# Reading each tile's head stacks in two halves instead of one piece, in the cross-attention of a decoder layer

## The chip, the cores and the metric

The kernel runs on one core of a Trainium2 chip. The metric is the device time of one execution in microseconds, as the median of several runs. TensorE does matrix products and transposes, VectorE, ScalarE and GpSimd (POOL in the profile) work element by element, and SyncE (SP) issues every transfer between the chip's memory (DRAM scratch arrays here) and SBUF.

## The reference, cut to what matters

One decoder layer on x of 16 x 256 x 512 in float32: a windowed self-attention, a cross-attention with a context of the same shape, and a mixture of experts. The change lies in the cross-attention:

```python
x = x + _L0_xattn_ref(_layernorm(x, axis=-1), ctx_2048, ctx_2048, L0_xattn_gamma)

def _L0_xattn_ref(q, k, v, gamma):
    N_HEAD = 8
    B, Dq, Lq = q.shape            # 16, 256, 512
    h = N_HEAD
    dq = Dq // h                   # 32
    qh = q.reshape(B, h, dq, Lq)
    kh = k.reshape(B, h, dq, Lk)
    vh = v.reshape(B, h, dv, Lk)
    qk = jnp.einsum('bhdq,bhdl->bhql', qh, kh) * scale
    sm = jax.nn.softmax(qk, axis=-1)
    ret = jnp.einsum('bhql,bhdl->bhdq', sm, vh)
    return gamma * ret.reshape(B, Dv, Lq)
```

The position axis (256) plays the part of the channels: a head is 32 rows of a sequence, and the scores of a head are a 512 x 512 matrix.

## The kernel before

The stage works on 32 tiles of 128 rows by 512 columns, which are four heads each (XPT = 4, XD = 32). A float32 product is made of rounded parts: ScalarE rounds queries and keys (`q_round`, `k_round`), GpSimd forms the rests (`q_rest`, `k_rest`), and rounded part and rest lie in `qp` and `kp`. To contract all products of the parts in one matmul, the parts of a head's 32 rows are stacked on 96 partitions. That move goes through DRAM: `write_queries` and `write_keys` write a tile's parts to `sq_scratch` and `sk_scratch` (512 KB each), and `read_stacks` reads them back into `qst` and `kst`, [partitions, 4 heads, 512], in six transfers of 256 KB; each writes 32 of the partitions, every third one, for all four heads. There are three stack buffers (STACKS = 3). Rows 96 and 97 of `qst` take the negated maxima of the scores, also as part and rest, which `max_rows` copies there in two transfers of 8 KB.

TensorE makes every score twice. `scores` (L782) makes them for the maxima, which VectorE takes (L928); `transposed_scores` (L791) makes them again, transposed, with the maxima subtracted by the two extra rows, and ScalarE takes their exponentials (L868). `weigh` (L802) multiplies by the values `vt`, and `sums` (L812) adds up the denominators. The loop on TensorE runs over steps, four to a tile, and four heads or chunks to a step; the scores run six steps (AHEAD = 6) ahead of the transposed scores. So the scores of tile n+2, first head, stand at the middle of tile n, and those of its third head at the start of tile n+1. Behind the first scores of tile n+2 in the same queue stand the transpose of the maxima of tile n+1 (L819) and all the rest of tile n. Only the first scores of a tile wait for the stacks:

```python
if h == 0 and q == 0:
    pe.wait_ge(s_st[m % STACKS], 16 * 2 * PARTS * (m // STACKS + 1))
```

SyncE issues its transfers in one order, and each waits for its turn in that order. For tile n of the loop this is: `read_stacks(n + 2)`, when the writes of that tile have landed and the transposed scores of tile n-1 are done (this frees the buffer); `write_queries(n + 3)`, `write_keys(n + 3)`, `load_values(n + 2)`, `load_context(n + 4)` (`cin`), `load_x(n + 5)`, and last `max_rows(n + 1)`, which waits for ScalarE's `xmhi` (L889). The transposed scores of tile n+1 wait for these rows at the tile's start.

Of the kernel before, what the change touches and what calls it, by code (L numbers as in the profile page):

```python
# [5 lines left out]
F32 = mybir.dt.float32  # L6
# [586 lines left out]
def cross_attention(nc, x1, ctx_in, ctx_t, gamma, sq, sk, mv2, mv3, x2, cst):  # L593
# [4 lines left out]
    with ctx:  # L598
        def sb(name, shape, dt):
            return ctx.enter_context(nc.sbuf_tensor(name, shape, dt))  # L600
# [4 lines left out]
        def sem(name):  # L605
            return ctx.enter_context(nc.semaphore(name))

        PARTS = 3
        KS = PARTS * XD
# [3 lines left out]
        STACKS = 3  # L613
# [11 lines left out]
        qst = [sb(f"qst{i}", [P, XPT, D], F32R) for i in range(STACKS)]  # L625
        kst = [sb(f"kst{i}", [P, XPT, D], F32R) for i in range(STACKS)]
# [20 lines left out]
        s_qn, s_qhi, s_qlo = sem("x_qn"), sem("x_qhi"), sem("x_qlo")  # L647
        s_khi, s_klo = sem("x_khi"), sem("x_klo")
        s_qw, s_kw = sem("x_qw"), sem("x_kw")
        s_st = [sem(f"x_st{i}") for i in range(STACKS)]  # L650
        s_row = [sem(f"x_row{i}") for i in range(STACKS)]
        s_ones = sem("x_ones")
        s_sc, s_mx = sem("x_sc"), sem("x_mx")
# [14 lines left out]
        def tile(n):  # L668
            return 0 <= n < TILES

        @block.sync
        def _(sp):
            sp.dma_start(gam[:, :], gamma.rearrange("(a b) -> a b", a=1).broadcast_to([P, 1])).then_inc(s_gam, 16)

            def load_x(m):
                sp.dma_start(x2[:, m, :], x1v[m // 2, m % 2]).then_inc(s_xi[m % 6], 16)

            def load_context(m):
                if m >= 4:
                    sp.wait_ge(s_klo, m - 3)  # L680
                sp.dma_start(cin[:, m % 4, :], cv[m]).then_inc(s_ci[m % 4], 16)

            def load_values(m):
                if m >= 3:
                    sp.wait_ge(s_pv, CB * (m - 2))
                sp.dma_start(vt[:, m % 3, :, :], ctx_t[m]).then_inc(s_vt[m % 3], 16)

            def write_queries(m):
                sp.wait_ge(s_qlo, m + 1)
                sp.dma_start(sq[m % 2].rearrange("h p d -> p h d"), qp[m % 2][:, :, :].bitcast(F32)).then_inc(s_qw, 16)  # L690

            def write_keys(m):
                sp.wait_ge(s_klo, m + 1)
                sp.dma_start(sk[m % 2].rearrange("h p d -> p h d"), kp[m % 2][:, :, :].bitcast(F32)).then_inc(s_kw, 16)

            def read_stacks(m):
                sp.wait_ge(s_qw, 16 * m + 16)
                sp.wait_ge(s_kw, 16 * m + 16)
                if m >= STACKS:
                    sp.wait_ge(s_ts, 16 * (m - STACKS) + 16)  # L700
                qv = sq[m % 2].rearrange("h (j r) d -> h r j d", j=XPT)
                kv = sk[m % 2].rearrange("h (j r) d -> h r j d", j=XPT)
                for c in range(PARTS):
                    rows = slice(c, KS, PARTS)
                    sp.dma_start(qst[m % STACKS][rows, :, :].bitcast(F32), qv[c // 2]).then_inc(s_st[m % STACKS], 16)
                    sp.dma_start(kst[m % STACKS][rows, :, :].bitcast(F32), kv[c % 2]).then_inc(s_st[m % STACKS], 16)

            def max_rows(m):
                for k, (part, here) in enumerate(((mhi, s_mhi), (mlo, s_mlo))):
                    sp.wait_ge(here, m + 1)  # L710
                    row = qst[m % STACKS][KS + k:KS + k + 1, :, :].rearrange("o h (q n) -> o (h q) n", n=P)
                    sp.dma_start(row.bitcast(F32), part[:, :].bitcast(F32)).then_inc(s_row[m % STACKS], 16)

            for m in range(4):
                load_x(m)
                load_context(m)
            load_x(4)
            for n in range(-3, TILES):
                if tile(n + 2):
                    read_stacks(n + 2)  # L720
                if tile(n + 3):
                    write_queries(n + 3)
                    write_keys(n + 3)
                if tile(n + 2):
                    load_values(n + 2)
                if n >= 0 and tile(n + 4):
                    load_context(n + 4)
                if n >= 0 and tile(n + 5):
                    sp.wait_ge(s_qn, n + 2)
                    load_x(n + 5)  # L730
                if tile(n + 1):
                    max_rows(n + 1)
# [41 lines left out]
        @block.tensor  # L774
        def _(pe):
            def scores(g, q):
                m, h = g // CB, g % CB
                if h == 0 and q == 0:
                    pe.wait_ge(s_st[m % STACKS], 16 * 2 * PARTS * (m // STACKS + 1))
                if 4 * g + q >= 2:  # L780
                    pe.wait_ge(s_mx, 4 * g + q - 1)
                nc.tensor.matmul(SC[q % 2][:, :], qst[m % STACKS][0:KS, h, q * P:(q + 1) * P],  # L782
                                 kst[m % STACKS][0:KS, h, :], start=True, stop=True).then_inc(s_sc, 1)

            def transposed_scores(s, h):
                n, c = s // CB, s % CB
                if c == 0 and h == 0:
                    pe.wait_ge(s_row[n % STACKS], 32 * (n // STACKS + 1))
                if 4 * s + h >= 2:
                    pe.wait_ge(s_exp, 4 * s + h - 1)  # L790
                nc.tensor.matmul(ST[h % 2][:, :], kst[n % STACKS][0:KM, h, c * P:(c + 1) * P],  # L791
                                 qst[n % STACKS][0:KM, h, :], start=True, stop=True).then_inc(s_ts, 1)

            def weigh(s):
                n, c = s // CB, s % CB
                pe.wait_ge(s_exp, 4 * s + 4)
                pe.wait_ge(s_vt[n % 3], 16 * (n // 3 + 1))
                if c == 0:
                    pe.wait_ge(s_oe, n)
                for h in range(XPT):  # L800
                    rows = slice(XD * h, XD * (h + 1))
                    last = nc.tensor.matmul(OB[rows, :], vt[:, n % 3, c, rows], prt[s % RING][:, h, :],  # L802
                                            start=(c == 0), stop=(c == CB - 1))
                last.then_inc(s_pv, 1)

            def sums(n, k):
                pe.wait_ge(s_add, XPT * (2 * n + k + 1))
                if k == 0 and n >= 2:
                    pe.wait_ge(s_on, n - 1)
                for h in range(XPT):  # L810
                    rows = slice(XD * h, XD * (h + 1))
                    last = nc.tensor.matmul(SU[n % 2][rows, :], ones[:, :], prt[(CB * n + 2 * k) % RING][:, h, :],  # L812
                                            start=(k == 0), stop=(k == 1))
                last.then_inc(s_su, 1)

            def max_transposes(n):
                pe.wait_ge(s_mx, 16 * n + 16)
                pe.wait_ge(s_mlo, n)
                nc.tensor.transpose(MX[0:XPT * CB, 0:P], nmx[:, n % 2, :], ident[:, :]).then_inc(s_mt, 1)  # L819

            pe.wait_ge(s_ones, STACKS + 1)
            for s in range(FIRST, LAST):
                for i in range(XPT):
                    if 0 <= s + AHEAD < STEPS:
                        scores(s + AHEAD, i)
                    if 0 <= s < STEPS:
                        transposed_scores(s, i)
                    if i == 1 and s % CB == 2 and tile(s // CB + 1):
                        max_transposes(s // CB + 1)
                    if i == 1 and 0 <= s - 1 < STEPS:  # L830
                        weigh(s - 1)
                if s % CB in (0, 2) and tile(s // CB - 1):
                    sums(s // CB - 1, s % CB // 2)
# [597 lines left out]
```

## Time and profile before

| | |
|---|---|
| time, median of 3 runs | 2736.11 us (2734.95 to 2745.65) |
| profiled execution | 2744.02 us, its span 2742.3 us, mean granted clock 0.976 |
| TensorE matmuls busy | 2591.8 us, 95% of the span |
| VectorE, ScalarE, GpSimd busy | 65%, 35%, 31% of the span |
| cross-attention, 1984 to 2512.5 us | 528.5 us: TensorE 499.8 busy, VectorE 409.3, GpSimd 408.1, ScalarE 362.1; transfer engines busy 0.62, 198 GB/s |

Read the table from below: the stage is a fifth of the time, every engine in it is under its full load, and TensorE is nearest to it. The durations in the trace come from the one profiled execution, which was 8 us longer than the median of the others.

### The profile page before, as it was taken

What the parts mean: (1) busy time and instruction counts of PE and PEld (TensorE: products, weight loads), DVE (VectorE), ACT (ScalarE), POOL (GpSimd) and SP (SyncE); (2) the same over time, 40 slices, a digit from 0 to 9 for tenths busy, and PEclk for the clock granted to TensorE, in tenths of its full rate; (3) what the DMA queues carried; (4) which work ended last, traced back from release to release, by engine and by line L of the source; (5) the groups of instructions that cost most, each with busy time, mean ns of one, the idle gap of its engine ahead of it and who ended that gap; (6) DMA issues with size and microseconds to landing.
All of it is one profiled execution on the core that took longest, in us unless ns stands there. A gap on an engine that the chain in (4) does not pass through costs nothing. (4 is left out here: it accounts for less than half of the span.)

```text
span 2742.3 us, 37159 instructions
## 1 busy us (share of the span) xinstructions
PE 2591.8 (95%) x12936; PEld 1920.3 (70%) x12936; DVE 1794.3 (65%) x3705; ACT 968.3 (35%) x2435; POOL 861.5 (31%) x698
## 2 busy tenths in 40 slices
PE   6999999999999999999999999999499999999794
PEld 5888888888888888888887888888343333333583
DVE  5777776655665566565565666566478777776657
ACT  2322223322222332222232222222257776776220
POOL 3211112321111222121132212111258888887000
PEclk9999999999999999999999999999789999999897
DMA  3123323222211222221122321110466666662003
GB/s 115 62 81 103 111 91 123 77 77 92 93 62 62 97 74 86 99 77 62 62 100 70 101 99 62 62 62 32 140 200 213 211 214 202 204 198 71 20 1 123
DMA packets 167078, 280.58 MB, mean 102 GB/s; under 512 B 12016, under 2 KB 78576, under 8 KB 166896
## 3 DMA queue, kind: packets, MB, share of 16 engines
q1 hardware_dynamic: 166896, 278.21, 30.3%
q8 instruction: 107, 1.75, 0.3%
q14 instruction: 75, 0.61, 0.1%
HBM read 185.37 MB, written 92.27 MB: 101 GB/s over the span
## 5 line engine op out<-in xcount | busy, mean ns | idle before, releaser
L324 PE MATMUL pj<-xnt,whi 128*128 128x512 f32 x2048 | 706.9, 407 | 4.4 <-DVE xnt L558 4.4
L417 ACT ACTIVATE pr<-sc,nmx 128x128 f32<-128x128 f32 (+1 forms) x512 | 211.1, 417 | 930.0 <-DVE nmx L503 930.0
L269 POOL TENSOR_TENSOR qt<-rot,swp 128x512 f32<-128x512 f32 x128 | 166.0, 1297 | 1107.8 <-DVE swp L483 1107.8
L324 PEld LDWEIGHTS pj<-xnt,whi 128*128 128x128 f32 x2048 | 387.5, 189 | 97.6 <-DVE xnt L558 5.2
L928 DVE TENSOR_REDUCE xnmx<-xsc 128x1 f32<-128x512 f32 x512 | 336.4, 684 | 125.5 <-PE xsc L782 122.1
L324 PE MATMUL pj<-xnt,wlo 128*128 128x512 f32 x1024 | 400.2, 391 | 0.0
L321 PE MATMUL pj<-whi,xnt 128*128 128x512 f32 x1024 | 352.8, 406 | 4.0 <-issue 4.0
L752 POOL TENSOR_TENSOR xprt<-xprt 128x512 f32<-128x512 f32 x256 | 320.2, 1283 | 103.6 <-PE xob L802 103.6
L868 ACT ACTIVATE xprt<-xst 128x512 f32<-128x512 f32 x512 | 291.8, 596 | 158.0 <-PE xst L791 156.7
L481 DVE TENSOR_TENSOR rot<-pj,trig 128x512 f32<-128x512 f32 x256 | 176.7, 690 | 213.7 <-PE pj L324 213.7
L782 PE MATMUL xsc<-kst,qst 96*128 96x512 f32 x512 | 241.6, 476 | 56.7 <-DMA kst<-sk_scratch 51.7
L782 PEld LDWEIGHTS xsc<-kst,qst 96*128 96x128 f32 x512 | 99.5, 195 | 265.9 <-DVE xnmx L928 184.2
L269 POOL TENSOR_TENSOR kt<-rot,swp 128x512 f32<-128x512 f32 x128 | 165.1, 1290 | 308.1 <-DVE swp L483 308.1
L512 DVE TENSOR_SCALAR pr<-pr,rinv 128x128 f32<-128x128 f32 (+1 forms) x512 | 253.2, 535 | 9.0
L503 DVE TENSOR_REDUCE nmx<-sc 128x1 f32<-128x128 f32 (+1 forms) x512 | 158.3, 351 | 146.3 <-PE sc L358 141.9
L321 PEld LDWEIGHTS pj<-whi,xnt 128*128 128x128 f32 x1024 | 193.2, 189 | 50.5 <-issue 4.3
L324 PEld LDWEIGHTS pj<-xnt,wlo 128*128 128x128 f32 x1024 | 194.9, 190 | 34.7
L345 PE MATMUL pj<-whi,ohi 128*128 128x512 f32 x512 | 212.4, 415 | 1.4 <-DVE olo L517 1.4
L791 PE MATMUL xst<-qst,kst 98*128 98x512 f32 x512 | 209.7, 412 | 3.0 <-ACT xprt L868 1.4
L491 DVE TENSOR_TENSOR xio<-pj,xio 128x512 f32<-128x512 f32 x128 | 88.5, 692 | 180.6 <-PE pj L345 180.6
L345 PE MATMUL pj<-whi,olo 128*128 128x512 f32 x512 | 201.6, 394 | 0.0
L321 PE MATMUL pj<-wlo,xnt 128*128 128x512 f32 x512 | 199.8, 390 | 0.0
(183 smaller groups left out, 4230.6 us busy)
## 6 DMA issues: line engine op xcount, KB each, us to landing
xnt<-xt_scratch SPq DMA_DIRECT2D x48, 1024.0 KB, 7.0
x_scratch<-xio SPq DMA_DIRECT2D x64, 512.0 KB, 3.6
xio<-x_scratch SPq DMA_DIRECT2D x48, 512.0 KB, 4.0
qst<-sq_scratch SPq DMA_DIRECT2D x96, 256.0 KB, 4.2
kst<-sk_scratch SPq DMA_DIRECT2D x96, 256.0 KB, 4.7
raw<-in_w_all_dram SPq DMA_DIRECT2D x64, 256.0 KB, 4.7
xt_scratch<-xnt SPq DMA_DIRECT2D x16, 1024.0 KB, 8.9
sq_scratch<-qp SPq DMA_DIRECT2D x32, 512.0 KB, 6.1
```

The source lines that it names most:

```text
L269: nc.gpsimd.tensor_tensor(qk["QK".index(kind)][h][:, :, :].rearrange("p b n -> p (b n)"), rot[r % 2][:, :], swp[r % 2][:, :], ALU.add).the ...
L321: last = nc.tensor.matmul(bank[:, :], moving[:, i * P:(i + 1) * P], wpart[:, w, :], start=(k == 0), stop=(k == 3 * CB - 1))
L324: last = nc.tensor.matmul(bank[:, :], wpart[:, w, i * HD:(i + 1) * HD], moving, start=(k == 0), stop=(k == 3 * CB - 1))
L345: last = nc.tensor.matmul(PJ[n % 3][:, :], o[:, h, tok], w[:, CH_O + h, :], start=(h == 0 and k == 0), stop=(h == HG - 1 and k == 2))
L417: nc.scalar.activation(pr[:, a % 4, lo:hi], SC[a % 2][:, lo:hi], ACT.Exp, bias=nmx[:, a % 4, t:t + 1], accum_out=rsum[:, a % 4, t:t + 1]). ...
L481: nc.vector.tensor_tensor(ro, bank, table(slice(0, P), q), ALU.mult)
L512: nc.vector.tensor_scalar(pr[:, a % 4, lo:hi], pr[:, a % 4, lo:hi], rinv[:, a % 4, t:t + 1], None, ALU.mult).then_inc(s_pr, 1)
L752: nc.gpsimd.tensor_tensor(a[:, h, :], a[:, h, :], b[:, h, :], ALU.add).then_inc(s_add, 1)
L782: nc.tensor.matmul(SC[q % 2][:, :], qst[m % STACKS][0:KS, h, q * P:(q + 1) * P], kst[m % STACKS][0:KS, h, :], start=True, stop=True).then_ ...
L791: nc.tensor.matmul(ST[h % 2][:, :], kst[n % STACKS][0:KM, h, c * P:(c + 1) * P], qst[n % STACKS][0:KM, h, :], start=True, stop=True).then_ ...
L868: nc.scalar.activation(prt[s % RING][:, h, :], ST[h % 2][:, :], ACT.Exp).then_inc(s_exp, 1)
L928: nc.vector.tensor_reduce(nmx[:, m % 2, k:k + 1], SC[q % 2][:, :], AX.X, ALU.max, negate=True).then_inc(s_mx, 1)
```

## The change

`read_stacks` takes two halves of two heads each. A half is read in six transfers of 128 KB, twelve for a tile, and each half of each buffer has a semaphore of its own. `scores` waits for the first half at the first head of a tile and for the second at the third head. The bytes, their places and the size of a contiguous piece (512 values) stay.

```diff
-        s_st = [sem(f"x_st{i}") for i in range(STACKS)]
+        s_st = [[sem(f"x_st{i}{k}") for k in range(2)] for i in range(STACKS)]
...
-                for c in range(PARTS):
-                    rows = slice(c, KS, PARTS)
-                    sp.dma_start(qst[m % STACKS][rows, :, :].bitcast(F32), qv[c // 2]).then_inc(s_st[m % STACKS], 16)
-                    sp.dma_start(kst[m % STACKS][rows, :, :].bitcast(F32), kv[c % 2]).then_inc(s_st[m % STACKS], 16)
+                for k in range(2):
+                    heads, here = slice(2 * k, 2 * k + 2), s_st[m % STACKS][k]
+                    for c in range(PARTS):
+                        rows = slice(c, KS, PARTS)
+                        sp.dma_start(qst[m % STACKS][rows, heads, :].bitcast(F32), qv[c // 2][:, heads, :]).then_inc(here, 16)
+                        sp.dma_start(kst[m % STACKS][rows, heads, :].bitcast(F32), kv[c % 2][:, heads, :]).then_inc(here, 16)
...
-                if h == 0 and q == 0:
-                    pe.wait_ge(s_st[m % STACKS], 16 * 2 * PARTS * (m // STACKS + 1))
+                if h % 2 == 0 and q == 0:
+                    pe.wait_ge(s_st[m % STACKS][h // 2], 16 * 2 * PARTS * (m // STACKS + 1))
```

SyncE's queue in the steady state, before: the end of one tile's reads (32 partitions x 4 heads x 512), what stands behind them, and the first reads of the next tile. The names in brackets are the semaphores that a transfer waits for; `x_ts` counts transposed scores, `x_mhi` and `x_mlo` the maxima.

```order
L705 DMA qst<-sq_scratch 32x4x512
L706 DMA kst<-sk_scratch 32x4x512
L690 DMA sq_scratch<-qp 128x2x512 [waits x_qlo]
L694 DMA sk_scratch<-kp 128x2x512 [waits x_klo]
L686 DMA vt<-in_ctx_t_dram 128x512 [waits x_pv]
L681 DMA cin<-in_ctx_in_dram 128x512 [waits x_klo]
L676 DMA x<-x_scratch 128x512 [waits x_qn]
L712 DMA qst<-xmhi 1x16x128 [waits x_mhi]
L712 DMA qst<-xmlo 1x16x128 [waits x_mlo]
L705 DMA qst<-sq_scratch 32x4x512 [waits x_ts,x_kw,x_qw]
L706 DMA kst<-sk_scratch 32x4x512
```

The same place in the changed kernel:

```order
L707 DMA qst<-sq_scratch 32x2x512
L708 DMA kst<-sk_scratch 32x2x512
L690 DMA sq_scratch<-qp 128x2x512 [waits x_qlo]
L694 DMA sk_scratch<-kp 128x2x512 [waits x_klo]
L686 DMA vt<-in_ctx_t_dram 128x512 [waits x_pv]
L681 DMA cin<-in_ctx_in_dram 128x512 [waits x_klo]
L676 DMA x<-x_scratch 128x512 [waits x_qn]
L714 DMA qst<-xmhi 1x16x128 [waits x_mhi]
L714 DMA qst<-xmlo 1x16x128 [waits x_mlo]
L707 DMA qst<-sq_scratch 32x2x512 [waits x_ts,x_kw,x_qw]
L708 DMA kst<-sk_scratch 32x2x512
```

The order is the same, but twelve reads of two heads stand where six of four heads stood, so everything from the query write on has six more issues ahead of it.

TensorE's queue at the start of a tile, before (L782 scores, L791 transposed scores, L802 weighting; `x_row0` are the two copied rows of maxima):

```order
L782 MATMUL xsc<-kst,qst 128x512 [waits x_mx]
L791 MATMUL xst<-qst,kst 128x512 [waits x_exp,x_row0]
L782 MATMUL xsc<-kst,qst 128x512 [waits x_mx]
L791 MATMUL xst<-qst,kst 128x512 [waits x_exp]
L802 MATMUL xob<-xprt,vt 32x512 [waits x_vt2,x_exp]
```

The same place in the changed kernel, where every line number is two higher:

```order
L784 MATMUL xsc<-kst,qst 128x512 [waits x_mx,x_st11]
L793 MATMUL xst<-qst,kst 128x512 [waits x_exp,x_row0]
L784 MATMUL xsc<-kst,qst 128x512 [waits x_mx]
L793 MATMUL xst<-qst,kst 128x512 [waits x_exp]
L804 MATMUL xob<-xprt,vt 32x512 [waits x_vt2,x_exp]
```

Nothing moves on TensorE. The scores of the third head of a tile, which stand directly ahead of the transposed scores that open another tile, have a wait of their own now (`x_st11` is the second half of buffer 1).

## Rows read from the trace of the kernel before

**Rows 1.** The page: TensorE's busy tenths in 40 slices of the span.

```profile
PE   6999999999999999999999999999499999999794
```

**Rows 2.** Waits from 2012 to 2500 us: total us, times, longest.

```profile
PE xsc L782 <- DMA kst<-sk_scratch: 22.1, 28, 2.3
```

**Rows 3.** Timeline of TensorE: start, duration, instruction [idle time before it <- what ended it].

```profile
2210.26 0.50 PE L782 MATMUL xsc<-kst,qst 96*128 96x512 f32 x1 [0.33 <-DMA kst<-sk_scratch]
...
2218.37 0.39 PE L791 MATMUL xst<-qst,kst 98*128 98x512 f32 x1
...
2227.23 0.50 PE L782 MATMUL xsc<-kst,qst 96*128 96x512 f32 x1 [1.14 <-DMA kst<-sk_scratch]
...
2259.77 0.48 PE L782 MATMUL xsc<-kst,qst 96*128 96x512 f32 x1 [0.18 <-DVE xnmx L928]
...
2277.89 0.53 PE L782 MATMUL xsc<-kst,qst 96*128 96x512 f32 x1 [2.29 <-DMA kst<-sk_scratch]
...
2295.46 0.50 PE L782 MATMUL xsc<-kst,qst 96*128 96x512 f32 x1 [0.20 <-DMA kst<-sk_scratch]
...
2328.91 0.50 PE L782 MATMUL xsc<-kst,qst 96*128 96x512 f32 x1 [1.33 <-DMA kst<-sk_scratch]
```

**Rows 4.** Windows: length, busy by engine, granted clock, DMA share, GB/s.

```profile
2278.20:2281.60 3.40, 3.40 (x13) 1.00 (x11) 1.38 (x2) 1.20 (x2) 3.40 (x4) 0.50 0.40 155
2261.40:2264.80 3.40, 3.40 (x23) 1.39 (x16) 1.84 (x5) 1.57 (x4) 3.40 (x4) 1.00 0.61 229
```

**Rows 5.** Timeline of SyncE's queue over one tile: start of an issue, its duration.

```profile
2201.91 0.61 SPq L705 DMA_DIRECT2D qst<-sq_scratch  x1
...
2205.13 0.60 SPq L706 DMA_DIRECT2D kst<-sk_scratch  x1
2205.78 0.59 SPq L690 DMA_DIRECT2D sq_scratch<-qp  x1
2207.06 0.38 SPq L694 DMA_DIRECT2D sk_scratch<-kp  x1
2207.48 1.39 SPq L686 DMA_DIRECT2D vt<-in_ctx_t_dram  x1
2208.91 1.17 SPq L681 DMA_DIRECT2D cin<-in_ctx_in_dram  x1
2210.13 0.49 SPq L676 DMA_DIRECT2D x<-x_scratch  x1
2214.03 0.56 SPq L712 DMA_DIRECT2D qst<-xmhi  x1
2214.64 0.59 SPq L712 DMA_DIRECT2D qst<-xmlo  x1
...
2218.06 0.61 SPq L705 DMA_DIRECT2D qst<-sq_scratch  x1
```

**Rows 6.** Waits of SyncE's queue, 2012 to 2500 us.

```profile
SPq L712 <- ACT xmhi L889: 123.2, 29, 6.8
```

**Rows 7.** Windows of 2 us of the same tile, columns as in rows 4.

```profile
2201.90:2203.90 2.00, 1.95 (x8) 0.89 (x12) 2.00 (x4) 2.00 (x6) 2.00 (x3) 1.00 0.18 41
2203.90:2205.90 2.00, 2.00 (x16) 0.84 (x12) 1.90 (x5) 1.24 (x4) 2.00 (x3) 1.00 1.01 296
...
2211.90:2213.90 2.00, 2.00 (x16) 0.83 (x12) 0.88 (x2) 0.85 (x3) 2.00 (x3) 1.00 1.02 391
2213.90:2215.90 2.00, 2.00 (x16) 0.82 (x12) 1.61 (x4) 1.08 (x4) 2.00 (x3) 1.00 0.07 21
```

**Rows 8.** Transfers from 2012 to 2500 us: size, median us from issue to landing.

```profile
kst<-sk_scratch SPq DMA_DIRECT2D x87, 256.0 KB, 4.7
...
qst<-xmlo SPq DMA_DIRECT2D x29, 8.0 KB, 1.9
```

**Rows 9.** Timeline of SyncE's queue at the start of the stage.

```profile
1960.09 0.42 SPq L681 DMA_DIRECT2D cin<-in_ctx_in_dram  x1
```

**Rows 10.** Timeline of TensorE: the first scores of the stage.

```profile
1983.71 1.19 PE L782 MATMUL xsc<-kst,qst 96*128 96x512 f32 x2 [29.67 <-DMA kst<-sk_scratch]
```

## The prediction, made before the changed kernel ran

> **What bounds the kernel now.** I read the page first: TensorE is busy nearly everywhere, the cross-attention too [rows 1]. So only what makes TensorE stand still there, or lowers its clock, is worth time. The changed transfers exist only in that stage, and everything ahead of and behind it stays as it is.
>
> Next the waits between 2012 and 2500 us, where the stage is in its steady state. TensorE's matmuls stand still for one thing worth naming: scores (L782) that wait for the stacks, 22.1 us in 28 waits, 0.79 us each, at the first scores of a tile [rows 2].
>
> Then the timeline, one row per such place. Tile starts lie 16.97 us apart with a wait of 1.14 us at the end (2210.26 to 2227.23), so 15.83 us of work [rows 3]. Where the stacks were there in time, 0.18 us remained, charged to VectorE (2259.77). That is the floor: the wait can't fall below it. After the wait of 2.29 us at 2277.89 the next interval is 17.57 us, less its own wait of 0.20 still 17.37, so 1.54 us more than 15.83. The windows say why: from 2278.2 to 2281.6 the granted clock was 0.50 (the 1.2 GHz level) and TensorE retired 13 matmuls in 3.4 us, against 23 at 1.00 in an equal stretch of the tile before [rows 4]. The clock fell likewise behind the wait of 1.33 us at 2328.91 [rows 3] and behind one of 1.51 us at the stage's start: three times in all, each about 3.4 us long.
>
> Last SyncE's queue, for one tile. Let T be the issue of a tile's first stack read, 2201.91. The sixth is at T+3.2, one per 0.645 us; the query write at T+3.9, the key write at T+5.2, vt, cin and x up to T+8.7, then the queue idles until xmhi exists at T+12.1, and the next reads go at 2218.06 [rows 5]. SyncE waits 123.2 us in 29 waits for xmhi, 4.2 us per tile: that is the room in the queue [rows 6]. TensorE wants the first scores at about T+8.0 (2210.26 less 0.33) and gets them at T+8.3. The transfer engines carry almost nothing until T+2.0, are full from there to T+12.0, at 296 GB/s with stack reads in them and at 391 with the writes and plain loads behind them, and idle after it (share 0.07) [rows 7].
>
> **The change, step by step.**
>
> *First half earlier.* Today 1.57 MB are asked for within 3.9 us, 400 GB/s, and delivered at about 296, so the sixth read queues behind five others: issued at T+3.2, landed at T+8.3. The new first half is also six issues. No row shows a stack read of 128 KB. Its issue lies between 0.33 and 0.60 us: a plain load of 256 KB took 0.42 us on an empty queue and an 8 KB row copy 0.56 [rows 5, 9]; I take 0.60, since the small row copy hardly costs less than a large read. Then 128 KB per 0.645 us is 203 GB/s, under what the transfer engines deliver, and nothing queues. Data starts about 1.9 us after an issue (the engines are empty until T+2, and 8 KB land in 1.9 us [rows 7, 8]), takes 0.45 us at 296 GB/s and is signalled about a microsecond later: T+3.2+3.4 = T+6.6 at the latest likely, T+5.5 with quick issues. Both are ahead of T+8.0. The wait goes, down to the floor: 22.1 - 28 x 0.18 = **17.1 us**. A hiccup like the one at 2277.89 (2 us late) would still leave only some 0.5 us.
>
> *Clock.* With no wait over a microsecond in the middle of a tile the three slow stretches have no cause: 3 x 1.54 = **4.6 us**. Bounds 0 (they come anyway) and 4.6.
>
> *Second half.* Issued to T+7.7, landed near T+10.6. Scores of the third head are wanted eight scores later, half a tile, T+15.9 (the added wait stands right there, with transposed scores and weighting queued behind it). Free by 5 us.
>
> *What is queued behind on SyncE.* Six more issues of 0.645 us: 3.9 us, bounds 0.6 (twelve of 0.33 + 0.045 against 3.9) and 3.9. The key write also waited for GpSimd, 2207.06 instead of 2206.4, and now finds kp ready. vt and cin took 1.39 and 1.17 us to issue while the transfer engines were full and 0.42 when they were empty [rows 5, 9]; how much of that comes back I leave at nothing to 1.7 us. SyncE is then done with x at T+10.2 to T+12.2. xmhi exists at about T+11.3 (T+12.1 less the removed wait). The row copies are issued at most 1 us late.
>
> *What is queued behind on the transfer engines.* The stack reads end at T+7.7+1.9 = T+9.5 in place of about T+7.4; 1.84 MB of writes and loads at 400 GB/s take 4.6 us, so all is drained at **T+14.1** where it was T+12.0. The row copies now go into queues that are still full and land near T+15.2; today they land at 2214.64+1.9 = T+14.6 [rows 5, 8]. The transposed scores of the next tile want them at 15.83+0.3 = **T+16.1** (2218.37 against the reads at 2218.06 [rows 3, 5]). Margin 0.9 us; landings of today scatter by about that, so I book 0.07 us a tile, **2 us**. The key write, issued at T+8.4, has 1.05 MB ahead and in it: T+9.5+2.6+1.2 = T+13.3, and the next reads need it at T+15.8. cin lands near T+15 and is rounded in the next tile, behind exponentials of its first step, past T+16. Free.
>
> *Start of the stage.* The very first scores wait until 1983.71 for six whole reads [rows 10]; they come 1.7 us sooner. But each next tile's reads there wait for a write that is now issued 3.9 us later (by as much, less some of the queueing), so tile 1 starts no sooner, and the first row copies queue behind a write. Bounds -1.7 and +4; I take **+1 us**.
>
> Sum: -17.1 - 4.6 + 2 + 1 = -18.7 us on the profiled 2744.0, 2725.3 or -0.68%. The median of the runs shown is 8 us below the profiled run, and I can't tell whether it had the three slow stretches; without them the gain is 14.1. On the median I take **17 us, 2719**.
>
> **A rule against it.** The rows show 8 KB landing after 1.9 us and whole reads, six in flight, after 4.7 [rows 8]: small ones are not slow here. The Trainium skill (DMA: Bandwidth & Descriptors, section Bandwidth) says to batch transfers to 1 MiB and more, and gives 0.95 us of busy transfer time for 64 KB against 6.15 for 1 MB. An estimate between its figures is 2.0 us for 256 KB and 1.3 for 128 KB, so 3.6 us more per tile if they ran one after the other; the drain would come at about T+15.6 and the rows half a microsecond late. By that the gain would be some 4 us only. The trace speaks against it: six reads landed 8.3 us after the first issue, not twelve.
>
> **The rivals.**
>
> *A. The rows are late, and it is slower (chance 0.14).* Each half costs the transfer engines far more than half a read, so they stay full from T+2 on. Place: the wait of the transposed scores for the row copies. It decides from a landing at T+16.9 on (T+16.1 plus the 0.77 us a tile gained), that is a drain 1.7 us after my T+14.1, or stack reads at about 170 GB/s. If a half cost as much as a whole, 0.88 us, reads would take 10.6 us, the rows land at T+18.2 and tiles last 17.9 us where they last 15.83+0.79 = 16.6: 29 x 1.3, about +38 us. At 160 GB/s the rows land at T+17.5 and the tile is 17.2 us: +17 us, 2753. For it: 2 KB packets into 32 partitions already run at 296 where others run at 400. Against: the packets keep their size.
>
> *B. The rows take back part (0.20).* Lands between T+16.2 and T+16.8: 0.1 to 0.6 us a tile, 3 to 17 us; 2722 to 2736, most near 2729.
>
> *C. The stacks are no sooner (0.06).* Landing is latency and not queueing: then the first half still comes at T+3.2+4.7 = T+7.9, and the gain is 0 to 6 us: 2730 to 2736. The 1.9 us of the row copies speak against it.
>
> *D. The forecast (0.60):* 2712 to 2725.
>
> **Numbers.** The range 2711 to 2738 holds D, B and C and leaves A. What a measurement can tell from no change is about 0.5%, 13.7 us, so faster means below 2722.4: most of D (0.51) and a little of B, 0.53; slower means above 2749.8: most of A, 0.12; between them 0.35.
>
> **What would show it.** The matmul wait for the stacks falls from 22.1 us to under 6; stack reads land in about 3.4 us; SyncE's reads keep a pitch of 0.6 to 0.65 us; its wait for xmhi shrinks from 4.2 to under 1 us; the row copies land later than 1.9 us; the interval of tiles is 16.0 us; no stretch at half clock from 2012 to 2500. Wrong if transposed scores (L791 before) wait for row copies at tile starts, if the halves' pitch is over 0.75 us, or if stack reads land no sooner.

## The result and the profile after

The changed kernel took 2724.77 us (median of 5 runs, 2723.01 to 2726.1) against 2736.11 us before (median of 5, 2733.56 to 2745.65): a ratio of 0.9953, 95% interval 0.9937 to 0.9969. It is faster by 11.3 us, a little under half a per cent. The profiled executions are further apart: 2725.4 us (span 2723.6) against 2744.0, which is 18.6 us. The prediction called it faster below 2722.4 us, with a chance of 0.53; the time fell just above that, where the chance of 0.35 lay.

The waits between 2012 and 2500 us, the view of [rows 2] for the changed kernel (line numbers are two higher, so L784 are the scores and L793 the transposed scores):

```profile
PE xsc L784 <- DVE xnmx L930: 10.2, 60, 0.5
...
PE xst L793 <- DMA qst<-xmlo: 2.0, 4, 1.0
```

No wait of TensorE for the stacks is left in the stretch, neither at the first nor at the third head; it was 22.1 us. What remains ahead of the scores are 60 waits of 0.17 us put down to VectorE, half of them at the first head of a tile and half at the third, where the kernel before had none. The second kind costs nothing that can be seen: a tile lasts 16.03 us, as it does with four stack buffers (below), which has them at the first head alone. A new wait has come, 2.0 us in all, for the copied rows of maxima.

SyncE's queue over one tile, the view of [rows 5], from T = 2195.24:

```profile
2195.24 0.60 SPq L707 DMA_DIRECT2D qst<-sq_scratch  x1
...
2202.28 0.60 SPq L708 DMA_DIRECT2D kst<-sk_scratch  x1
2202.92 0.59 SPq L690 DMA_DIRECT2D sq_scratch<-qp  x1
...
2206.25 0.50 SPq L676 DMA_DIRECT2D x<-x_scratch  x1
2207.25 0.56 SPq L714 DMA_DIRECT2D qst<-xmhi  x1
2207.85 0.59 SPq L714 DMA_DIRECT2D qst<-xmlo  x1
2211.27 0.60 SPq L707 DMA_DIRECT2D qst<-sq_scratch  x1
```

A read of half the bytes takes as long to issue, 0.60 us, one per 0.64. The query write goes at T+7.7 where it went at T+3.9, the rows at T+12.0, and the next reads after 16.03 us. Half a microsecond is left between the end of the x issue and the rows; it was 3.4. SyncE's waits for xmhi in the stretch fell from 123.2 us to 30.0, and 14.4 of these are a single wait.

The transfers of the same stretch, as in [rows 8], size and median us to landing:

```profile
kst<-sk_scratch SPq DMA_DIRECT2D x174, 128.0 KB, 2.6
...
qst<-xmlo SPq DMA_DIRECT2D x31, 8.0 KB, 3.3
```

The reads land in 2.6 us where they took 4.7; the rows land in 3.3 us where they took 1.9. Both come from the load on the transfer engines, and the windows of 2 us show it (columns of [rows 4], the third figure from the right is the clock, the last the GB/s):

```profile
2195.20:2197.20 2.00, 1.85 (x8) 0.86 (x12) 1.95 (x4) 2.00 (x6) 2.00 (x3) 1.00 0.21 70
2197.20:2199.20 2.00, 2.00 (x16) 0.84 (x12) 1.97 (x5) 1.24 (x4) 2.00 (x3) 1.00 0.66 193
...
2201.20:2203.20 2.00, 2.00 (x12) 0.70 (x7) 1.74 (x3) 1.65 (x4) 0.96 (x1) 1.00 0.75 208
...
2205.20:2207.20 2.00, 2.00 (x16) 0.83 (x12) 0.73 (x2) 0.93 (x4) 2.00 (x3) 1.00 1.03 351
2207.20:2209.20 2.00, 2.00 (x16) 0.83 (x12) 1.69 (x4) 1.08 (x4) 2.00 (x3) 1.00 1.01 331
2209.20:2211.20 2.00, 1.99 (x12) 0.68 (x4) 1.17 (x3) 1.45 (x4) 1.56 (x2) 1.00 0.23 82
```

While the halves are read the transfer engines are two thirds busy at 193 to 208 GB/s; before, they were full at 296 GB/s in the same place. Nothing queues, so a read lands soon. The writes and loads come later, so the engines are still full when the rows are asked for, at T+12.0 and T+12.6, and idle from about T+14.4.

### The profile page after: what moved, and what is told of

Its sections match the earlier page's. It is cut to its first block and busy times, and to the rows that moved or that the text cites. A ratio compares the mean times of both kernels' runs of the same rounds, so it can differ in the third digit from the quotient of the medians.

```text
span 2723.6 us, 37383 instructions
## 1 busy us (share of the span) xinstructions
PE 2586.9 (95%) x12936; PEld 1918.0 (70%) x12936; DVE 1794.5 (66%) x3705; ACT 964.9 (35%) x2435; POOL 861.5 (32%) x698
## 5 line engine op out<-in xcount | busy, mean ns | idle before, releaser
L784 PE MATMUL xsc<-kst,qst 96*128 96x512 f32 x512 | 238.6, 470 | 39.9 <-DMA kst<-sk_scratch 27.4
L784 PEld LDWEIGHTS xsc<-kst,qst 96*128 96x128 f32 x512 | 99.1, 194 | 247.6 <-DVE xnmx L930 172.2
L793 PE MATMUL xst<-qst,kst 98*128 98x512 f32 x512 | 208.8, 411 | 4.9 <-DMA qst<-xmlo 2.9
```

## The experiments

Ratios are to the kernel before, run beside each kernel on the same chip; "stage" is the time from the first scores to the start of the last transposed scores in the profiled execution.

| kernel | median us | before, same chip | ratio, 95% interval | stage us |
|---|---|---|---|---|
| before, unchanged | 2738.57 | 2741.0 | 0.9989, 0.998 to 0.9998 | 543.0 |
| halves, one signal | 2800.68 | 2741.0 | 1.022, 1.0205 to 1.0236 | 603.3 |
| three parts | 2809.47 | 2741.0 | 1.0248, 1.0234 to 1.0262 | 617.3 |
| writes between the halves | 2721.09 | 2741.0 | 0.9929, 0.9916 to 0.9941 | 527.0 |
| smaller rings (control) | 2733.41 | 2739.56 | 0.9985, 0.9973 to 0.9996 | 538.0 |
| four stack buffers | 2722.34 | 2739.56 | 0.9939, 0.9923 to 0.9954 | 527.2 |
| second half before the rows | 2722.31 | 2739.56 | 0.9935, 0.9917 to 0.9954 | 529.2 |
| changed kernel again | 2724.98 | 2738.6 | 0.9949, 0.9931 to 0.9967 | 529.8 |
| writes between, again | 2720.35 | 2738.6 | 0.993, 0.9911 to 0.9949 | 527.4 |
| four stack buffers, again | 2720.9 | 2738.6 | 0.9932, 0.9914 to 0.9949 | 528.4 |

The stage was 548.4 us in the first trace of before and 530.5 in that of the changed kernel. (The stretch of 528.5 us in the table of the kernel before ends at 2512.5 us; the last transposed scores start at 2532.1.) The stage as measured here leaves out how long the first scores wait for their reads; that comes under the reasons below. The first row is a yardstick too: the same kernel against itself came out at 0.9989, so a difference of a part in a thousand, 2.7 us, is not to be read in this table.

**The kernel before, traced once more.** No edit. 

> The kernel before, unchanged, for a second trace of it. The first trace, of an execution of 2744.0 us, lies 8 us over the median, and the changed kernel gained 18.7 us on it but 11.3 us on the median. Theory: the waits for the stacks are about the same in every execution (17 to 24 us in 28 waits between 2012 and 2500 us), and it is the slow stretches of TensorE's clock behind some of them (three, 4.6 us) that come and go; so an execution near the median shows none or one. Rival: the waits themselves vary from run to run, and a quick execution shows 8 to 15 us of them.

Measured: the profiled execution took 2734.0 us, and in the same stretch:

```profile
PE xsc L782 <- DMA kst<-sk_scratch: 18.1, 25, 2.4
```

18.1 us of waits, and no stretch at half clock in 2012 to 2500 us, where the first trace had 22.1 us and three. The stage was 5.4 us shorter and began 4.1 us sooner. The theory holds as to the clock; the waits differ by 4 us too. So the loss by slow stretches is a loss of some executions. The two traces lie on either side of the middle: the first, on which the sum was made, was of a long execution, this one of the quickest of its ten (median 2738.57).

**One signal for both halves.** The twelve smaller reads stay, and the first head waits for all of them, so what is taken away is the first half's own signal.

```diff
-                if h % 2 == 0 and q == 0:
-                    pe.wait_ge(s_st[m % STACKS][h // 2], 16 * 2 * PARTS * (m // STACKS + 1))
+                if h == 0 and q == 0:
+                    for k in range(2):
+                        pe.wait_ge(s_st[m % STACKS][k], 16 * 2 * PARTS * (m // STACKS + 1))
```

> The changed kernel with its twelve transfers of 128 KB, but the scores of a tile's first head wait for both halves (as before, one point of waiting a tile). Theory (what counts is that the first half is signalled by itself): the twelfth read is issued 7.0 us after the first and lands 2.6 us later, at T+9.6 to T+10; TensorE wants it at T+8.0, so it stands 1.6 to 2 us in each of 28 tiles, 45 to 56 us, and slow stretches of the clock of 1.5 us each come behind some of them: 2765 to 2815 us. Rival (small transfers alone bring it, since nothing queues): 2723 to 2730 us, with waits under 6 us.

Measured 2800.68 us, 59.7 us above the kernel before. The wait is where the theory puts it, and the reads land as in the changed kernel:

```profile
PE xsc L785 <- DMA kst<-sk_scratch: 55.1, 26, 2.9
...
qst<-sq_scratch SPq DMA_DIRECT2D x156, 128.0 KB, 2.6
```

55.1 us in 26 waits, 2.1 us each. Twelve stretches at half clock, each 3.4 us, lie behind them; at 1.5 us each, an estimate from the three of the first trace, they make some 18 us more. Twelve smaller transfers under one signal cost 60 us here, since the twelfth is issued only 7.0 us after the first. The signal of the first half makes up for that loss and brings all of the gain.

**Three parts.** First head, second head, then two heads; a signal for each.

```diff
-                for k in range(2):
-                    heads, here = slice(2 * k, 2 * k + 2), s_st[m % STACKS][k]
+                for k, heads in enumerate((slice(0, 1), slice(1, 2), slice(2, 4))):
+                    here = s_st[m % STACKS][k]
```

> Three parts in place of two: first head, second head, third and fourth, six transfers each, eighteen a tile, a signal for each part. Theory (the price is SyncE's issue, about 0.64 us whatever the size, and the row copies behind it): eighteen reads take 11.5 us, what stands behind them 5 us, so the row copies are issued from T+15 on and land near T+19, and a tile lasts 18.5 to 19 us in place of 16.0: 2795 to 2815 us, with waits of the transposed scores for qst<-xmlo of 2.5 to 3 us a tile. Rival (bytes are what counts, the issue is cheap for smaller reads or hidden): 2720 to 2730 us.

Measured 2809.47 us, inside the expected 2795 to 2815. The issue is the price: a read of 64 KB took 0.59 us to issue at the median, as one of 256 KB, and it landed in 2.2 us.

```profile
PE xst L793 <- DMA qst<-xmlo: 48.0, 16, 4.4
...
qst<-sq_scratch SPq DMA_DIRECT2D x157, 64.0 KB, 2.2
```

The shape of the loss was not as expected. It is not 2.5 to 3 us at each tile but 3.0 us at 16 places in 26 tiles, every other tile mostly: tiles of 16.0 us alternate with tiles of 20 to 22 us, and behind the long waits the clock is down. Timeline of SyncE's queue over a long tile, and two windows of TensorE around its end:

```profile
2197.37 0.51 SPq L707 DMA_DIRECT2D qst<-sq_scratch  x1
...
2213.48 0.57 SPq L714 DMA_DIRECT2D qst<-xmhi  x1
2214.09 0.59 SPq L714 DMA_DIRECT2D qst<-xmlo  x1
2214.79 0.52 SPq L707 DMA_DIRECT2D qst<-sq_scratch  x1
```

```profile
2214.00:2218.00 4.00, 0.00 (x0) 0.00 (x0) 1.28 (x2) 0.49 (x1) 3.23 (x3) 0.69 0.74 246
2218.40:2222.40 4.00, 4.00 (x13) 1.50 (x14) 1.30 (x2) 1.60 (x3) 1.27 (x1) 0.51 0.38 98
```

SyncE issues with no wait for 17.4 us, longer than a tile of 16.0: it is itself what bounds the long tile. The late rows hold TensorE back by some 4 us, and with that lead SyncE is in time for the next tile, so every other tile is short: over the stretch SyncE still stands 49 us in 35 waits. The rows are asked for 16.1 us after the tile's first read. TensorE starts no matmul from 2214 to 2218, and then runs 13 in 4 us at a granted clock of 0.51.

**Writes between the halves.** First half, writes of queries and keys, second half; one wait keeps the scratch from being overwritten.

```diff
             def write_queries(m):
                 sp.wait_ge(s_qlo, m + 1)
+                if m >= 2:
+                    sp.wait_ge(s_st[(m - 2) % STACKS][1], 16 * 2 * PARTS * ((m - 2) // STACKS + 1))
...
                 if tile(n + 2):
-                    read_stacks(n + 2)
+                    read_stacks(n + 2, 0)
                 if tile(n + 3):
                     write_queries(n + 3)
                     write_keys(n + 3)
+                if tile(n + 2):
+                    read_stacks(n + 2, 1)
```

> The changed kernel with the writes of queries and keys issued between the two halves, so that the first reads and the writes stand in the queue where they stood before; the write of the queries waits also for the second half of two tiles earlier, which has long landed. Theory: in the steady state nothing changes (tiles of 16.0 us; second half landed by T+13, wanted at T+15.9), at the start of the stage the reads of tile 1 begin about 3 us sooner and the first row copies are not late: 1 to 3 us less than the changed kernel, 2721.5 to 2724. Rival (the row copies and the second half then queue behind the writes on the transfer engines, and the second half comes late): waits at L782's third head or for qst<-xmlo, 2728 to 2745 us.

Measured 0.9929 of the kernel before, and beside the changed kernel on one chip 2720.35 against 2724.98 us: 4.6 us less, somewhat more than expected. What the traces show of it lies at the start of the stage. The changed kernel's timeline of TensorE there:

```profile
1995.60 1.22 PE L784 MATMUL xsc<-kst,qst 96*128 96x512 f32 x2 [0.45 <-DMA kst<-sk_scratch]
...
2003.73 0.80 PE L793 MATMUL xst<-qst,kst 98*128 98x512 f32 x1 [0.95 <-DMA qst<-xmlo]
```

And the same two places in the kernel before:

```profile
1996.39 1.30 PE L782 MATMUL xsc<-kst,qst 96*128 96x512 f32 x2 [0.28 <-DVE xnmx L928]
...
2003.28 0.63 PE L791 MATMUL xst<-qst,kst 98*128 98x512 f32 x1
```

With the writes between, neither wait is there (one of 0.5 us, in the repeat of 0.3 us, for the second half of tile 0 has come), and the steady waits for the rows (5.2 us on the weight-load side in the second trace of the changed kernel) are down to 1.7 us in the repeat, which follows.

> The writes between the halves, again, beside the changed kernel on the same chip. If the start of the stage gains, 1 to 3 us below the changed kernel, with the stage (first scores to last transposed scores) at 527 us against 530.5. Rival: the two are the same within 1 us, and the lower time came from the chip it ran on.

The stage of 527.4 against 529.8 and 530.5 us agrees. The traced execution of the changed kernel was the quickest of its six, 2.1 us below their median. So the two traces are only 2.2 us apart, and from the first scores to the third transpose of the maxima the kernel with the writes between is 2.2 us quicker (43.2 against 45.4). The rest of the 4.6 us is in no trace and stays open.

**Four stack buffers, and its control.** Six whole reads and one signal, as before the change. The memory comes from one buffer less for the exponentials and two less for the context, which the control has as well.

```diff
-        RING = 6
-        STACKS = 3
+        RING = 5
+        STACKS = 4
...
-        cin = sb("cin", [P, 4, D], F32)
+        cin = sb("cin", [P, 2, D], F32)
```

> Control for the next kernel: the kernel before (six transfers of 256 KB, three stack buffers) with five in place of six buffers for the exponentials and two in place of four for the context, loads of the context issued later at the start. These give the memory that a fourth stack buffer takes. Expected of either theory: like the kernel before, 2732 to 2742 us, with the waits for the stacks at about 0.6 to 0.8 us a tile.

> The control with four stack buffers, six whole transfers of 256 KB and one signal. The reads no longer wait for the transposed scores of the tile before to free a buffer; SyncE issues them behind the row copies, about 3 us sooner. Theory (the waits are the time between a freed buffer and a landed read, too long by 0.3 to 2.3 us; either an earlier start or a shorter landing removes them): waits for the stacks under 6 us, tiles of 16.0 us, no slow stretch, row copies landed in 1.9 us: 12 to 20 us less than the control, 2717 to 2725 us, at least as good as the halves. Rival (splitting itself is what helps, the start is bound by something else such as the landing of the writes): the reads start hardly sooner, waits stay above 15 us, 2730 to 2740 us.

Measured: control 2733.41, four buffers 2722.34 us on the same chip, 11.1 us less, a little under the 12 to 20 expected. The control still waits; TensorE's matmuls have no wait for stacks or rows in the stretch at all with four buffers. The first row is of the control, the other two of the four buffers (transfers, then a wait of SyncE's queue):

```profile
PE xsc L782 <- DMA kst<-sk_scratch: 13.4, 24, 1.3
```

```profile
kst<-sk_scratch SPq DMA_DIRECT2D x87, 256.0 KB, 4.5
```

```profile
SPq L711 <- ACT xmhi L889: 154.3, 31, 14.4
```

The reads land hardly faster than before (4.5 us, it was 4.7); they start sooner, right behind the rows, and that is enough. So the stall was the distance from a freed buffer to landed stacks, and splitting is one of two cures. This one also leaves SyncE its room, 4.7 us a tile beside the one long wait of 14.4, and the rows land in 1.8 us.

> The four whole stack buffers again, beside the others. Steady tiles of 16.03 us as with the halves and a stage of 527 us, so 1 to 3 us below the changed kernel. Rival: the smaller rings for exponentials and context cost 1 to 3 us elsewhere, and it is level with it.

It came to 2720.9 us, 4.1 us below the changed kernel, and level with the writes between. Where the 4.1 us lie is not shown: the two traced executions are 0.6 us apart (2722.23 and 2722.87), the stage of 528.4 us is longer than the 527 expected, and its first scores come 8.6 us after the first read, as in the kernel before, where the changed kernel has 5.9.

**Second half behind writes and loads, just ahead of the rows.** The edit moves `read_stacks(n + 2, 1)` down to there.

> The changed kernel with the second half read behind the writes and the loads, just ahead of the row copies. Theory: first half and writes as early as before the change; the second half is issued from about T+7.5 to T+11.5 and lands near T+14, wanted at T+15.9; the start of the stage gains as in the kernel with the writes between: 2720 to 2725 us. Rival (the loads now run into the second half and it lands after T+16): waits of the third head's scores for the stacks, 0.5 to 2 us a tile, 2740 to 2780 us.

Measured 2722.31 us, ratio 0.9935: the theory as to the time and the steady tiles of 16.03 us. The gain at the start did not come with it. There the third head's scores of tile 0 wait for the second half, and the stage took 529.2 us, not 527:

```profile
1990.32 1.22 PE L788 MATMUL xsc<-kst,qst 96*128 96x512 f32 x2 [1.60 <-DMA kst<-sk_scratch]
```

The order of what stands behind the first half hardly matters, as long as all of it is issued before the rows are due.

**The changed kernel again.** 

> The changed kernel, unchanged, beside the two variants that came out lowest, all on one chip. Steady tiles of 16.0 us and row copies that land in about 3 us again. Theory (the changed kernel repeats itself within about 3 us, the kernel before scatters over 10 us, since its waits and slow clock stretches vary): 2722 to 2727 us against a kernel before at 2734 to 2742, a ratio of 0.993 to 0.9965. Rival (the first comparison was right to the tenth of a per cent): the ratio is 0.995 to 0.996 again.

Measured 2724.98 us (2722.87 to 2729.51) against 2738.6 (2733.46 to 2749.32), 0.9949. The changed kernel repeats its 2724.8 within its scatter of 7 us, the kernel before scatters over 16 us. The two pairs, 0.9953 and 0.9949, agree within their intervals, so this does not decide between theory and rival; a gain of 11 to 14 us is what both say.

## Why the prediction came out as it did

The mechanism was right, and so was the time in its range: 2724.77 lies at the upper edge of the forecast of 2712 to 2725, which had been given 0.60, and within rival B's 2722 to 2736 too. So it is the traces and not the time that tell which of the two it was. They are cut here at the first stack read of the stage, the first scores, and the transposes of the maxima, one a tile (L819 before, L821 changed):

| stretch, us | before | before, second trace | changed | changed, second trace |
|---|---|---|---|---|
| first stack read to first scores | 8.6 | 8.5 | 5.9 | 5.9 |
| from there to the third transpose | 44.9 | 46.4 | 45.3 | 45.4 |
| third to last transpose, 29 tiles | 484.7 | 477.9 | 465.1 | 465.7 |
| from there to the last transposed scores | 18.8 | 18.7 | 20.0 | 18.8 |
| sum | 557.0 | 551.5 | 536.3 | 535.8 |

*First half earlier: right, in every part.* The pitch of issues stayed at 0.64 us, the engines were off their limit at 203 GB/s as worked out (193 to 208), the reads landed in 2.6 us (3.4 assumed) and the wait fell to the floor of 0.17 us. The kernel with one signal shows that it is the first half's own signal that does it, that with four buffers that only the time of arrival counts. Rival C, landing as pure latency, is out: 4.7 us became 2.6. On the trace that the sum was made from, the steady part came out as booked: the 29 tiles are 19.6 us shorter, and the terms were -17.1 - 4.6 + 2 = -19.7.

*Clock and waits: the terms that were mis-sized for the median.* The 4.6 us and the 17.1 us were booked from one trace, of a long execution. The second trace of the kernel before has none of the three slow stretches and 18.1 us of waits in place of 22.1, and against it the 29 tiles are 12.2 to 12.8 us shorter. On the median the gain measured 11.3 and 13.6 us, where I said 17. I had noted that the median might lack the slow stretches and took a middle value; the lower one, 14.1, was nearer. The reason given, that waits over a microsecond cause the slow stretches, is too simple: in the first trace waits of 1.42 us (2194.12) and 1.26 us (2480.28) had none behind them, and in the second a wait of 2.39 us had none. What decides it stays open.

*The row copies: right in kind, nearer than thought.* The drain was to be at T+14.1 and was at about T+14.4; the rows were to land at T+15.2 and landed at T+15.9 at the median (2207.85 less 2195.24, and 3.3 us), so of the margin of 0.9 us 0.2 was left. TensorE's matmuls waited for them 2.0 us in the steady stretch and 2.8 us in the second trace; I had booked 2. By the prediction's own list such waits were a sign of being wrong. They did come, four in the stretch, one at the start and one at the end, and they were small. The writes and loads ran at 351 and 331 GB/s at their end, where the 391 of before had been taken; why is not shown. Rival B is this mechanism, and it stayed at the small end. Rival A did not happen: the engines were 0.66 to 0.75 busy while the halves were read, and not full. The three parts came to A's late rows and to its time by another way, the eighteen issues.

*Start of the stage: booked +1, and it gained.* The parts that were named are there: the scores of tile 1 wait 0.45 us and the first transposed scores 0.95 us, and the reads of tile 1 began 13.0 us after those of tile 0 where it was 11.2. But the first scores came 2.7 us sooner after the first read (2.5 against the second trace of before), not 1.7. The first read and the first scores, before and changed:

```profile
1975.09 0.65 SPq L705 DMA_DIRECT2D qst<-sq_scratch  x1
```

```profile
1976.80 0.65 SPq L707 DMA_DIRECT2D qst<-sq_scratch  x1
```

```profile
1982.68 1.19 PE L784 MATMUL xsc<-kst,qst 96*128 96x512 f32 x2 [26.92 <-DMA kst<-sk_scratch]
```

Before, the scores stood at 1983.71 [rows 10]. From the first read to the third transpose it took 51.2 us, against 53.6 and 54.8 before: a gain of 2.3 us or more where a loss of 1 was booked. Not foreseen: the last tile's rows are late by 1.0 us too, with a slow stretch of the clock behind it in that one execution; in the second trace they are late by 0.9 us with none.

*What of the agreement was luck.* The sum gave 2725.3 us for the profiled execution, and it took 2725.4. The steady part earned that. The rest cancelled out: the start gained 2.3 us in place of losing 1, the end lost 1.3 us that nobody had booked, and the time ahead of the first stack read, which the change does not touch, was 1.7 us longer. That last time scatters, from 1971.2 to 1976.8 us in these four traces alone, and it is one reason why single executions can't be compared to the microsecond.

*The rule of larger transfers.* By an estimate between the figures that the Trainium skill gives (DMA: Bandwidth & Descriptors, section Bandwidth; they are for transfers issued from GpSimd, and this kernel issues from SyncE) halves would cost 3.6 us more of transfer time a tile; by that the gain was to be 4 us. The trace disagrees at 128 KB: the engines were two thirds busy while halves were read. With three parts the time did rise, but there the cost was SyncE's issue and not the transfer.

## What to carry to other kernels

Where an engine waits for a batch of transfers, look first at whether they queue (full transfer engines, landings that grow with the place in the batch) and which part the consumer needs first. Here a signal for that part brought the whole gain, and smaller pieces without it cost 2.2%. Asking for the whole batch sooner, into a spare buffer, did as well. Then add up the issues on the queue against the interval: at 0.6 us an issue, for 64 KB as for 256, twelve left half a microsecond of room and eighteen were too many, and whatever small urgent transfer stands last pays for it. Take a loss that depends on the run, as slow clock stretches do, from two traces.

## What the runs showed of the hardware

- Issuing a strided read on SyncE took 0.6 us at the median for 256 and 128 KB and 0.59 for 64 KB; a plain load of 256 KB took 0.43 us on empty engines and 0.9 to 1.2 us at the median on full ones, at most 2.4. Single reads took 1.4 to 1.8 us now and then.
- Landings from these scratch arrays while the transfer engines were not full: 2.2 us for 64 KB, 2.6 us for 128 KB; six of 256 KB asked for within 3.9 us, which kept them full, landed in 4.2 us (`qst`) and 4.7 us (`kst`) at the median.
- Of 25 to 28 waits of up to 2.4 us one execution of the kernel before had three stretches of 3.4 us at the 1.2 GHz level behind them and another had none; with waits of 2.1 us on average there were twelve in 26. With three parts, idle times of 2.5 to 4.4 us mostly had stretches of 6.8 us behind them.
